# The last tiles' rows loaded into homes of their own, and the first routed rows queued ahead of the second expert's weights

## The reference

```python
sg = silu(jnp.einsum('bsd,fd->bsf', x, Wsg))          # FS = 704, shared expert
su = jnp.einsum('bsd,fd->bsf', x, Wsu)
shared_out = jnp.einsum('bsf,df->bsd', sg * su, Wsd)
logits = jnp.einsum('bsd,ed->bse', x, Wr)             # E = 8 experts
scores = jax.nn.softmax(logits, axis=-1)
topk_scores, topk_idx = jax.lax.top_k(scores, K)      # K = 2
w_full = jnp.sum(jax.nn.one_hot(topk_idx, E, dtype=x.dtype) * topk_scores[..., None], axis=-2)
g = silu(jnp.einsum('bsd,efd->bsef', x, Wg))          # F = 352
u = jnp.einsum('bsd,efd->bsef', x, Wu)
out_e = jnp.einsum('bsef,edf->bsed', g * u, Wd)
routed_out = jnp.einsum('bsed,bse->bsd', out_e, w_full)
return routed_out + shared_out
```

## Time and profile before

| what | value |
|---|---|
| time, median of 3 runs | 1725.35 us (1723.52 to 1727.61) |
| the profiled execution | 1726.2 us |
| its span in the profile | 1724.5 us |
| PE busy | 1642.5 us, 95% of the span |
| DVE, ACT, POOL busy | 1329.4, 766.8, 414.3 us |
| DMA, mean over the span | 195 GB/s |

### The profile page before, as it was taken

How to read it: one execution, slowest core, us unless ns; L and a number is a source line. 1 busy time by engine, 2 the same in 40 slices (tenths; PEclk the granted TensorE clock), 3 DMA queues, 4 the chain that set the end, 5 groups by cost and what they waited for, 6 DMA issues and landing times.

```text
span 1724.5 us, 26984 instructions
## 1 busy us (share of the span) xinstructions
PE 1642.5 (95%) x8813; PEld 1429.8 (83%) x8813; DVE 1329.4 (77%) x2559; ACT 766.8 (44%) x1132; POOL 414.3 (24%) x504
## 2 busy tenths in 40 slices
PE   5399999999989999999999997999999999999998
PEld 0278888888768888888888886999999999998897
DVE  4799999998689788888788773777777777775872
ACT  2343333334445555464545422555555555552321
POOL 0243444444222111322232341000000000005740
PEclk9699999999999999999999998999999999999999
DMA  8443232221454434555555687888878988776861
GB/s 327 111 155 98 73 97 79 91 91 67 166 167 146 166 141 141 194 192 196 195 185 177 226 283 260 268 290 283 284 266 277 299 293 282 258 237 194 283 213 37
DMA packets 139121, 335.82 MB, mean 195 GB/s; under 512 B 20584, under 2 KB 20584, under 8 KB 133376
## 3 DMA queue, kind: packets, MB, share of 16 engines
q1 hardware_dynamic: 109328, 248.65, 43.6%
q10 hardware_dynamic: 19440, 52.18, 8.3%
q0 software_dynamic: 10240, 33.56, 5.6%
HBM read 230.73 MB, written 103.60 MB: 194 GB/s over the span
## 4 chain that ended last, share of the span: by engine, by line
PE 78%; DVE 10%; DMA 5%; issue 3%; POOL 2%; ACT 2%; SPq 1%; DVEq 0%; ACTq 0%; POOLq 0%
PE bank L687 19%; PE bank L689 19%; PE bank L688 19%; PE bank L698 5%; PE bank L2321 5%; PE bank L2319 5%; PE bank L2320 5%; PE bank L2314 2%; DMA stage<-in_w_k 1%; DVE mix L1729 1%; POOL raw L1262 1%; DMA expert_in_rows<-y_rows 1%; DVE xm_lo L1735 1%; PE bank L2303 1%; DMA ex_x<-expert_in_rows 1%
## 5 line engine op out<-in xcount | busy, mean ns | idle before, releaser
L687 PE MATMUL bank<-gu_hi,ex_x_hl 128*128 128x352 f32 x1080 | 361.3, 335 | 0.1
L689 PE MATMUL bank<-gu_hi,ex_x_hl 128*128 128x352 f32 x1080 | 350.1, 324 | 0.0
L688 PE MATMUL bank<-gu_lo,ex_x_hl 128*128 128x352 f32 x1080 | 350.1, 324 | 0.0
L1262 POOL DMA_INDIRECT raw<-expert_out_rows,out_slots x64 | 77.1, 1204 | 540.0 <-DMA expert_out_rows<-y_rows 518.2
L687 PEld LDWEIGHTS bank<-gu_hi,ex_x_hl 128*128 128x128 f32 x1080 | 205.1, 190 | 0.4 <-issue 0.3
L688 PEld LDWEIGHTS bank<-gu_lo,ex_x_hl 128*128 128x128 f32 x1080 | 205.1, 190 | 0.0
L689 PEld LDWEIGHTS bank<-gu_hi,ex_x_hl 128*128 128x128 f32 x1080 | 204.7, 190 | 0.0
L1824 DVE TENSOR_TENSOR hid<-bank,sg_t 128x352 f32<-128x352 f32 x135 | 70.4, 521 | 124.8 <-PE bank L689 106.1
L2319 PE MATMUL bank<-dn_hi,hid_hi 128*128 128x512 f32 x405 | 161.3, 398 | 2.4 <-DVE hid_lo L1828 2.4
L2321 PE MATMUL bank<-dn_hi,hid_lo 128*128 128x512 f32 x405 | 159.6, 394 | 0.0
L2320 PE MATMUL bank<-dn_lo,hid_hi 128*128 128x512 f32 x405 | 158.5, 391 | 0.0
(11 more groups left out here) (256 smaller groups left out, 3826.3 us busy)
## 6 DMA issues: line engine op xcount, KB each, us to landing
raw<-in_ex_gu SPq DMA_DIRECT2D x40, 1408.0 KB, 6.5
raw<-in_ex_dn SPq DMA_DIRECT2D x40, 512.0 KB, 4.9
ex_x<-expert_in_rows SPq DMA_DIRECT2D x71, 256.0 KB, 6.2
expert_out_rows<-y_rows ACTq DMA_DIRECT2D x71, 256.0 KB, 5.9
h_rows<-h_t SPq DMA_DIRECT2D x64, 256.0 KB, 2.6
h_turned<-h_hl ACTq DMA_DIRECT2D x32, 512.0 KB, 3.0
ex_x_hl<-h_turned ACTq DMA_DIRECT2D x32, 512.0 KB, 3.9
x_t<-in_x SPq DMA_DIRECT2D x32, 256.0 KB, 2.7
```

Source lines behind the costliest of these rows:

```text
L687: pe.matmul(acc, act_hi[i], w_hi[i], start=(i == 0), stop=False)
L688: pe.matmul(acc, act_hi[i], w_lo[i], start=False, stop=False)
L689: last = pe.matmul(acc, act_lo[i], w_hi[i], start=False, stop=(i == chunks - 1))
L1262: pool.indirect_dma_start(rows[:, pair % 2, a, :], None, ys_d, bass.IndirectOffsetOnAxis(ap=out_slots[:, k, n:n + 1], axis=0)).then_inc(ar ...
```

## The change

The last eight tiles (24 to 31) all get homes in base: places 7, 8, 0, 1, 2, 3, 5, 6. SP loads them one after the other behind wait_a2, with no wait for a scatter, counted by two semaphores of four tiles each. POOL scatters them by scatter_last. On SP, pads 4 to 7 move behind gu(0)/dn(0), and gu(1)/dn(1) with their wait for SHIFTS_AT move behind load_rows(0) and load_rows(1), ahead of load_rows(2). turn_rows(0) moves on PE from ahead of turn_hid(36) to behind up(37); routed_x_hi(0) on ACT and x_lo(0) on DVE move behind the silu and the hidden product of unit 37.

```diff
+        LAST_HOME = {24: 7, 25: 8, 26: 0, 27: 1, 28: 2, 29: 3, 30: 5, 31: 6}
+
         def last_rows(n):
-            return base[:, n - 26, :] if n < 30 else sc_rows[:, n % 2, :]
+            return base[:, LAST_HOME[n], :]
...
             def load_last_scattered(n):
-                sp.dma_start(last_rows(n), h3_d[n * P:(n + 1) * P, :]).then_inc(sc_last_in[n // 30], 16)
+                sp.dma_start(last_rows(n), h3_d[n * P:(n + 1) * P, :]).then_inc(sc_last_in[int(n >= 28)], 16)
...
             wait_a2(sp)
-            for n in range(24, 26):
-                load_scattered(n)
-            for n in range(26, 30):
+            for n in range(24, NT):
                 load_last_scattered(n)
...
             for e in range(E // 2):
                 pad_rows(e)
-            for n in range(30, NT):
-                sp.wait_ge(sc_out[n % 2], 32 * 13)
-                load_last_scattered(n)
-            for e in range(E // 2, E):
-                pad_rows(e)
             sp.wait_ge(raw_pad, 2)
             sp.wait_ge(route_done, 1)
             load_gu(0)
             load_dn(0)
+            for e in range(E // 2, E):
+                pad_rows(e)
             for n in range(FU + 2, SPLIT):
                 load_residual(n)
-            sp.wait_ge(route_vec, SHIFTS_AT)
-            load_gu(1)
-            load_dn(1)
...
                 sp.wait_ge(pad_out[p], 16 * (E // 2))
-                sp.wait_ge(sc_out[p], 32 * 13)
-            sp.wait_ge(sc_last_out, 32 * (NT - 26))
-
-            for k in range(3):
+                sp.wait_ge(sc_out[p], 32 * 12)
+            sp.wait_ge(sc_last_out, 32 * (NT - 24))
+
+            for k in range(2):
                 load_rows(k)
+            sp.wait_ge(route_vec, SHIFTS_AT)
+            load_gu(1)
+            load_dn(1)
+            load_rows(2)
...
             def scatter_last(n):
                 pool.wait_ge(route_vec, (group_of(n) + 1) * ROUTE_OPS)
-                pool.wait_ge(sc_last_in[n // 30], 64 if n < 30 else 32)
+                pool.wait_ge(sc_last_in[int(n >= 28)], 64)
...
-            for n in range(24, 26):
-                scatter(n)
-            for n in range(26, NT):
+            for n in range(24, NT):
                 scatter_last(n)
...
                 hidhi(u - 1)
-                if u == ROUTED0 - 1:
-                    routed_x_hi(0)
                 for piece in HI_FIRST[u]:
...
                     load_turned(unit.n + 2)
+            routed_x_hi(0)
             act.wait_ge(h3T_out, 16 * NT)
...
                 hidlo_rows(u - 1)
-                if u == ROUTED0 - 1:
-                    x_lo(0)
                 pieces(BEFORE_HID, u)
...
+            x_lo(0)
             expert_lo(0, "dn")
...
                 if ROUTED0 <= u < LATE0 - 1:
                     turn_rows(u + 1 - ROUTED0)
-                elif u == ROUTED0 - 1:
-                    turn_rows(0)
                 turn_hid(u - 1)
                 up(u)
+                if u == ROUTED0 - 1:
+                    turn_rows(0)
```

## The result

| what | before | changed |
|---|---|---|
| median | 1725.54 us (6 runs) | 1716.83 us (6 runs) |
| ratio, 95% interval | 1 | 0.9946 (0.9928 to 0.9964) |
| profiled execution: time, span | 1726.2, 1724.5 us | 1715.77, 1714.0 us |

The ratio is a gain of 9.3 us (6.2 to 12.4), where 15.0 had been forecast; 1716.83 lies 1.3 us above the forecast's range. One of the six executions, 1834.7 us at a granted clock of 0.843, was disturbed and is left out of the ratio, and the median of the other five is 1715.81 us, 0.3 us above the range.

The account below looks back on a forecast made before the run. PE was taken as bound by its wait for rows(0) and the slow clock behind it. Terms 12.36 + 2.71 + 1.29 - 1.33 (wait, clock, hid_lo wait, new wait) make 15.0: 1725.35 - 15.0 = 1710.4 us, range 1708.0 to 1715.5.

Parts of the forecast that it names:

- the wait for rows(0): On PE ahead of turn_rows(0): unit 37 would begin at 1051.82 but starts at 1064.18; 12.36 us to go.
- the slow clock behind it: On PE from 1064.18 to 1073.54: granted clock 0.50, 9.36 us against 6.65 for the same work; 2.71 us to go.
- eight loads in a row: On SP from 1007.5, behind the last logits: tiles 24 to 31 issued about 0.43 us apart, done with two residuals by 1012.
- gu(0) near 1033.7: On SP: the first expert's load issued 1.2 us after route_done (1032.54), instead of at 1046.38.
- the new wait for x_lo(0): On PE ahead of turn_rows(1): x_lo(0) done at 1059.8, a wait of 1.33 us, bounds 0 and 2.5.
- the chain on ACT and DVE: From gu_hi(0) at 1053.0: 2.55, gu_lo(0) 3.09, hid(37) 0.45, x_lo(0) 0.69 us, so x_lo(0) done at 1059.8.
- the sum: At the start of down(37) on PE: 1064.4 instead of 1079.44, 15.0 us less, with everything later moving whole.
- I take 1.5 ... 1044.7: On SP's queue: a pad behind gu(0)/dn(0) lands at 1043.2, plus 1.5 us for scatters and ACT's loads: 1044.7.
- margin of some 2 us: Ahead of turn_rows(0) on PE: rows(0) lands at 1053 to 1054.5, some 2 us before PE needs it.
- supplies late: Rival, chance 0.27: rows(0) lands 1.5 us behind PE, gu(1) 3.5 later than ACT wants; gain 11.5 us, time 1713.9.
- The estimate of 2.2 us: SP's ring at half rate from 1033.7 to about 1038: gu(0)/dn(0) and all behind 2.2 us later instead of 1.5.
- The rivals of both other signs: Same, 0.03: waits return for rows(2), rows(3) or gu(2), 1722 to 1728. Slower, 0.03: pads delay gu(1) past 1075.2.

Follow-up runs that it names:

- pads first: Against the changed kernel, pads 4 to 7 are issued ahead of gu(0)/dn(0) instead of behind; ratio to the kernel before 0.9913.
- unchained pads: Against the changed kernel, no pad waits for the pad two before it, and pads 4 to 7 stay behind gu(0)/dn(0); ratio to the kernel before 0.9907.
- turn back: Against the changed kernel, turn_rows(0), x_hi(0) and x_lo(0) return to their places before the change; ratio to the kernel before 0.9945.
- pads first unchained: Against the changed kernel, all eight pads go ahead of gu(0)/dn(0) and none waits for another pad; ratio to the kernel before 0.9926.

## Why the prediction was right or wrong

*Right, by its own steps.* What bounded the kernel (the wait for rows(0) and the slow clock behind it), that the wait would go, eight loads in a row (1007.68), gu(0) near 1033.7 (1034.12), turn_rows(0) with its rows there (1056.51 against 1056.00; PE was 0.3 late before all of it), the new wait for x_lo(0) (0.67 and 0.88 against 1.33), and the chain on ACT and DVE. With supplies in time the sum holds: D falls by 14.99 with pads first, forecast 15.0. That it fits to 0.01 is luck: the new wait was some 0.5 shorter than summed and the steps around it together as much longer.

*Wrong: pad 4's landing, "I take 1.5 ... 1044.7".* It landed at 1048.28. The term was taken for two or three scatters left behind gu(0)'s issue; there were five, and the delay was 4.7 us instead of 1.5 (1048.28 - 1034.12, less the 9.5 that a pad behind the weights was to take). The scatters' start had been sized by landings of 2.4 to 7.6 us, of which 2.4 was a pad's and 7.6 a residual's; the homes' own loads took 8.1 to 10.0, and up to 8.1 in the kernel before already. That the scatters made pad 4 late is read from these landings, and from pads first, where gu(0) was issued when they were nearly through and took 6.4 us; no run took the scatters away.

From pad 4 on all is late. rows(0) was issued 2.7 us late, at 1053.12 (1050.4). gu(1) was issued 3.9 late, at 1055.88 (1052.0), and landed near 1063.5 (1058.3 to 1059.5). Some of this is a second, smaller slip: gu(1) follows rows(0) by 2.8 us, where 1.6 was summed; 0.6 of it was to be rows(1), which took 1.1, as it had in the kernel before. (Between pad 4 and rows(0) the forecast had some time to spare: by the terms named there pad 7 lands at 1048.9, not 1049.3, and the whole way took 4.8 us, not 5.7.) rows(0) had just used up its margin of some 2 us, gu(1) had overrun its own: ACT waited 2.81 us, PE 3.16. That was the rival "supplies late" (0.27), by its second half, with 3.1 us of its 3.5; its reason, that the scatters gain SP nothing, was not the one. The Trainium skill (DMA: Bandwidth & Descriptors, Queues, rings and completion order) says that each DMA engine goes round robin between the queue rows that have work. The trace agrees in direction: 9.2 us instead of 6.3 for gu(0). The estimate of 2.2 us that I had worked out by that rule was too low as well, since it let the scatters end at 1038; the last landed near 1047.3.

The table of SP's waits in the kernel before named an edge that I had priced too lightly, a pad that waits for the pad two before it:

```profile
SPq L1025 <- DMA expert_in_rows<-y_rows: 10.8, 3, 5.1
```

I wrote that pad 6 waits for pad 4, and counted its wait as pad 4's landing alone, without asking what it would be worth to have neither. The unchained pads show that with pad 4 as late as it was, this wait was nearly all of the loss on PE.

*Wrong: the range.* D fell by 11.87, the span by 10.5, the medians by 8.7. The late gu(1) accounts for 3.1 us of the shortfall; what lies beyond is within the interval of the gain, 6.2 to 12.4. Over the twelve profiles the start of turn_hid(35) lies between 1044.80 and 1047.47, and the stretch behind D between 640.61 and 644.91 us, the two profiles of the changed kernel at 643.93 and 640.61. From turn_rows(2) to the last y it is 472.7 to 472.8 us in all twelve; the difference is in the late units, where PE waits for hid while the results are gathered. PE's first such wait, and the stretch from 1560 to 1580 (granted clock, DMA share, GB/s are the last three), in the changed kernel:

```profile
1563.27 0.52 PE L2308 MATMUL bank<-ident,hid 128*128 128x128 f32 x3 [1.86 <-DVE hid L1819]
...
1560.00:1580.00 20.00, 18.10 (x95) 16.40 (x94) 15.58 (x20) 6.34 (x14) 15.73 (x15) 0.91 0.81 261
```

The same kernel again:

```profile
1561.91 0.52 PE L2308 MATMUL bank<-ident,hid 128*128 128x128 f32 x3 [1.65 <-DVE hid L1819]
...
1560.00:1580.00 20.00, 18.05 (x106) 16.51 (x105) 16.65 (x23) 6.82 (x15) 15.73 (x15) 1.00 0.92 317
```

In four of the twelve profiles (before, changed, turn back, pads first unchained) the granted clock fell to 0.5, the lower of its two levels, at the end of this wait or just behind it, where the wait was 1.9 to 2.2 us; in the other eight it stayed up behind 1.6 to 2.0 us. The stretch behind D took 642.8 to 644.9 us in the four and 640.6 to 642.1 in the eight; further waits for hid differ as well, so the clock need not be all of it. My range held the unknown costs of the change, but no term for this, which by these spreads moves a single execution by some 2 us; an estimate for a median of five is 1. With 1.4 us more on top the range would have held the time.

*The rivals of both other signs* did not come: no wait for rows returned later, and gu(1) was 3 us late, not 15. The clock did not fall behind the waits of 0.67 and 3.16 us in this stretch.

## What to carry to other kernels

When a DMA is moved behind a large one in a queue, look for every later instruction of that queue that waits for the moved one's landing, and price it as the large one's bytes plus a round trip during which the queue issues nothing: here that wait held SP for 9.9 us, and taking it away, or the pads out from behind the weights, gave back 3 us on PE. Once the first late supply is cured, the next one in the same queue decides, so give each supply its own time of need and its own margin. And size landings from rows of the same transfer with as much traffic as there will be, not from the range of other transfers.

## What was not expected of the hardware

A 1408 KB load took 6.3 us with the last scatter in flight beside it, 9.2 us beside indirect scatters issued every 1.28 us, and 6.0 and 7.6 us in the same place of the same kernel in two executions. And a PE wait of 3.16 us among full products left the clock up (matmuls 0.23 us apart behind it), while waits of 2.5 to 5.4 us for rows(0) were followed by slow ones (turn_rows(0) took 0.86 to 1.12 us instead of 0.60). Of the kernels run, pads first and pads unchained gained more than the changed one by their medians (1712.07 and 1710.3 us, each against its own runs of before); between these and the other kernels with D near 21 the times show no difference.
